# Output stage of a four-layer kernel: four tokens in a row per partition, and nine tiles for the chunks on their way out

## The reference

```python
y = (y0 + y1 + y2 + y3).transpose(0, 2, 1)
zf = jax.nn.silu(z.reshape(Bb, L, Cd))
yz = y * zf
mu = yz.mean(-1, keepdims=True)
xc = yz - mu
var = (xc * xc).mean(-1, keepdims=True)
yn = gamma * xc / jnp.sqrt(var + 1e-05) + beta
out = yn @ Wout
return out.reshape(Bb, H, W, -1)
```

## Time and profile before

| | |
|---|---|
| median of 3 runs | 3990.94 us (3986.17 to 3993.93) |
| the profiled execution | 3985.26 us, of it 3983.4 us span |
| TensorE busy, whole span | 3674.0 us (92%) |
| output stage, first transpose to last matmul | 3861.8 to 3977.4 us, 115.6 us |
| from there to the end of the span | 6.0 us |
| granted TensorE clock in the output stage | 0.99 |

### The profile page before, as it was taken

One profiled execution on the slowest core, in us unless ns is written; L12 is line 12 of the kernel. 1 busy time (PEld: TensorE's weight loads), 2 busy tenths in 40 slices (PEclk: granted clock), 3 DMA queues, 4 the chain that ended last, 5 costly groups with the idle time before them and its releaser, 6 DMA issues. The chain is left out here.

```text
span 3983.4 us, 72793 instructions
## 1 busy us (share of the span) xinstructions
PE 3674.0 (92%) x24602; PEld 2919.0 (73%) x24602; DVE 3250.2 (82%) x7827; ACT 2792.2 (70%) x6269; POOL 1342.3 (34%) x1652
## 2 busy tenths in 40 slices
PE   7999996999999999999999999998799866878898
PEld 5788774899888998889998898886576642333347
DVE  6899995777787777877778777776889988998885
ACT  5788884677776677767677766675967657777753
POOL 6799982000010000110001100003302348888873
PEclk8999997999999999999999999999999985887789
DMA  8777761000010000110001100003234446656567
GB/s 215 204 207 210 205 163 30 18 20 27 15 43 24 23 22 17 36 32 20 28 17 29 32 14 9 10 10 101 99 123 167 156 166 184 188 182 212 169 192 229
DMA packets 291428, 382.94 MB, mean 96 GB/s; under 512 B 43760, under 2 KB 162160, under 8 KB 290288
## 3 DMA queue, kind: packets, MB, share of 16 engines
q1 hardware_dynamic: 260288, 310.60, 25.6%
q0 software_dynamic: 29184, 67.27, 6.3%
q10 hardware_dynamic: 1584, 0.40, 0.1%
HBM read 205.46 MB, written 119.54 MB: 82 GB/s over the span
## 5 line engine op out<-in xcount | busy, mean ns | idle before, releaser
L959 ACT ACTIVATE l_ph<-l_T 128x512 fp32r<-128x512 f32 x1024 | 611.7, 597 | 550.4 <-PE l_T L864 550.4
L1076 DVE TENSOR_TENSOR l_pl<-l_T,l_ph 128x512 fp32r<-128x512 f32 x1024 | 707.2, 691 | 273.8 <-ACT l_ph L959 273.0
L1065 DVE CUSTOM_DVE_ANT_0 l_pr<-l_S,l_zero 128x512 f32<-128x512 f32 x1024 | 704.7, 689 | 76.4 <-PE l_S L787 12.7
L964 ACT ACTIVATE l_pr<-l_pr,l_st 128x512 f32<-128x512 f32 x1024 | 731.7, 715 | 1.1 <-DVE l_st L1071 1.0
L876 PE MATMUL l_O<-l_ph,l_vh 128*128 128x256 f32 x2048 | 661.6, 323 | 12.5 <-DVE l_pl L1076 12.1
L864 PE MATMUL l_T<-l_ident,l_pr 128*128 128x128 f32 x4096 | 612.8, 272 | 0.0
L1108 POOL TENSOR_TENSOR l_xs<-l_xs,l_bob 128x128 f32<-128x128 f32 x128 | 57.1, 460 | 1645.2 <-DMA l_xs<-x 1644.4
L864 PEld LDWEIGHTS l_T<-l_ident,l_pr 128*128 128x128 f32 x4096 | 507.8, 140 | 136.5 <-issue 0.2
L877 PE MATMUL l_O<-l_ph,l_vl 128*128 128x256 f32 x2048 | 577.9, 282 | 0.0
L878 PE MATMUL l_O<-l_pl,l_vh 128*128 128x256 f32 x2048 | 577.2, 282 | 0.0
L785 PE MATMUL l_S<-l_kh,l_qh 128*128 128x512 f32 x1024 | 417.7, 408 | 2.4 <-DVE l_st L1065 2.2
(11 more groups left out here) (269 smaller groups left out, 8025.9 us busy)
## 6 DMA issues: line engine op xcount, KB each, us to landing
l3b_u<-ub SPq DMA_DIRECT2D x256, 256.0 KB, 3.0
l_kq<-l_hl SPq DMA_DIRECT2D x192, 128.0 KB, 5.4
l_kq<-l_hl POOLq DMA_DIRECT2D x192, 128.0 KB, 4.5
zs<-l_tmp SPq DMA_DIRECT2D x64, 256.0 KB, 3.3
ub<-l3a_u SPq DMA_DIRECT2D x32, 512.0 KB, 3.4
l3b_z<-zs SPq DMA_DIRECT2D x64, 256.0 KB, 3.6
yz<-l3b_z SPq DMA_DIRECT2D x64, 256.0 KB, 3.3
l3b_dt<-yz SPq DMA_DIRECT2D x32, 512.0 KB, 4.8
```

What stands on the lines that cost most here:

```text
L959: e.activation(ph[:, i, :], psT[:, i, :], ACT.Copy).then_inc(p_hi, 1)
L964: e.activation(pr[:, s, es], pr[:, s, es], ACT.Exp, bias=st[:, s, 9:10], scale=SC, accum_out=st[:, s, 10 + k:11 + k]).then_inc(exped, 1)
L1065: e.tensor_tensor_reduce(pr[:, s, ks], psS[:, bk, :], zero[:].broadcast_to([128, 512]), 1.0, -3.0e38, ALU.add, ALU.max, st[:, s, kc:kc + 1 ...
L1076: e.tensor_tensor(pl[:, i, :], psT[:, i, :], f32(ph[:, i, :]), ALU.subtract).then_inc(p_lo, 1)
```

## The change

Three things change in the output stage.

- The four tokens of a partition become neighbours. Block j of a chunk is now the tokens j, 4 + j, 8 + j, ..., in place of 128j to 128j+127: both the transposes and the matmuls read the stationary operand as `j::4`.
- A partition's four tokens are then one row of 2 KB in `out`, and the store is 128 rows of 2 KB in place of 512 rows of 512 bytes.
- A chunk leaves from one of nine slots in place of three: three of `tE` and the six of `U` ("l3b_u"), which the scan steps have used up by then. The wait for a store, and the semaphores, go by nine.

```diff
-        M, B, N = 64 * NI, 6, 8 * NI
+        M, B, N, OUT = 64 * NI, 6, 8 * NI, 9
...
+        def o_of(f):
+
+            return tE[:, f % OUT, :] if f % OUT < 3 else U[:, f % OUT - 3, :]
...
-                    e.dma_start(out[n, 8 * c:8 * c + 8].rearrange("(t r) c d -> (r c) t d", r=2), tE[:, f % 3, :].rearrange("p (t c) -> p t c", t=4)).then_inc(o_out[f % 3], 16)
-            for i in range(3):
-                w.wait_ge(o_out[i], 16 * len(range(i, N, 3)))
+                    e.dma_start(out[n, 8 * c:8 * c + 8].rearrange("r (c t) d -> (r c) t d", t=4), o_of(f).rearrange("p (t c) -> p t c", t=4)).then_inc(o_out[f % OUT], 16)
+            for i in range(OUT):
+                w.wait_ge(o_out[i], 16 * len(range(i, N, OUT)))
...
-                            t = e.transpose(psL[:, 2 * (f % 2) + j // 2, 256 * (j % 2) + 128 * h:256 * (j % 2) + 128 * h + 128], y_of(f)[:, h, 128 * j:128 * j + 128], ident[:])
+                            t = e.transpose(psL[:, 2 * (f % 2) + j // 2, 256 * (j % 2) + 128 * h:256 * (j % 2) + 128 * h + 128], y_of(f)[:, h, j::4], ident[:])
...
-                            t = e.matmul(psC[:, f % 2, 128 * j:128 * j + 128], y_of(f)[:, h, 128 * j:128 * j + 128], gc[:, h, :], start=(h == 0), stop=(h == 1))
+                            t = e.matmul(psC[:, f % 2, 128 * j:128 * j + 128], y_of(f)[:, h, j::4], gc[:, h, :], start=(h == 0), stop=(h == 1))
...
-                    if f >= 3:
-                        w.wait_ge(o_out[f % 3], 16 * (f // 3))
+                    if f >= OUT:
+                        w.wait_ge(o_out[f % OUT], 16 * (f // OUT))
                     else:
                         w.wait_ge(added, M // 2)
                     for j in range(4):
-                        t = e.activation(tE[:, f % 3, 128 * j:128 * j + 128], psC[:, f % 2, 128 * j:128 * j + 128], ACT.Copy, scale=rs[:, f % 2, 2, j:j + 1])
+                        t = e.activation(o_of(f)[:, 128 * j:128 * j + 128], psC[:, f % 2, 128 * j:128 * j + 128], ACT.Copy, scale=rs[:, f % 2, 2, j:j + 1])
...
-                o = tE[:, f % 3, :].rearrange("p (t c) -> p t c", t=4)
+                o = o_of(f).rearrange("p (t c) -> p t c", t=4)
```

More of the change, by code:

```diff
@@ L1797, in y_of @@
             return tT[:, s:s + 2, :]
+        def o_of(f):
+            return tE[:, f % OUT, :] if f % OUT < 3 else U[:, f % OUT - 3, :]
         ident_in, wide_in, u_in, z_in, y_out = P.sem("ident_in"), P.sem("wide_in"), P.slots("u_in", 6), P.slots("z_in", 4), P.slots("y_out", 4)
         skips_in = P.slots("skips_in", 2)
-        weights, y_in, o_out = P.sem("weights"), P.slots("y_in", B), P.slots("o_out", 3)
+        weights, y_in, o_out = P.sem("weights"), P.slots("y_in", B), P.slots("o_out", OUT)
         d_full, C_full, X_full, W_full, T_full, O_full = (P.sem(x) for x in ("d_full", "C_full", "X_full", "W_full", "T_full", "O_full"))
```

## The result

The changed kernel takes 4048.07 us in the median of 4 runs against 3988.56 of the kernel before in 4: ratio 1.0142, 95% interval 1.0124 to 1.0159. That is 59.5 us slower, far outside the range of the prediction (3984 to 4020). The profiled execution has a span of 4040.5 us, 57.1 more than before.

The account below looks back on a forecast made before the run. TensorE was taken to bound the output stage, its loads as long as its matmuls. Nine tiles -6.8, 2 KB rows 0 and strided loads +19.2 gave +12.4 us on 3990.94, so 4003.3 us, range 3984 to 4020.

Parts of the forecast that it names:

- What bounds the stage: Output stage: TensorE sets the pace, busy 111.14 of 115.6 us; any slower plain load is paid at once.
- Nine tiles, -6.8 us: Output stage: nine tiles outlast any store, so the wait for it goes, worth up to -6.8 us.
- waiting for y: Chunk 31's y load: 2.0 us come back if TensorE stays as fast, none if strided loads slow it.
- 2 KB rows, 0: Output store: 128 rows of 2 KB land no sooner than 512 of 512 B; gain 0, bound half a us.
- The step that failed: Strided weight loads, output stage: L1984's strided moving rate, 1.04 ns a value, gives 133 ns a load; +19.2 us in all.
- The term of the plain loads: Output matmuls (L2034): 133 against 109 ns, +24 ns on each of 512 loads, 12.3 us.
- ScalarE's 0.85 ns on top of the plain rate: Upper bound for strided loads, from ScalarE's strided copy (L1686 against L1670): 108 ns a plain load, 70 us in all.
- The prediction's own sign, a spacing beyond 3 us: Output stage: group spacings passing 3 us would show the forecast wrong and the much slower case true.
- The term of the transposing loads: Output-stage transposes (L2025): 136 against 109 ns, +27 ns on each of 256 loads, 6.9 us.
- Rival D: Output-stage loads pay the price of ScalarE's strided copies: +70 - 6.8 = +63.6 us, 4054; chance 0.12.
- rival A: The forecast itself: strided output-stage loads at 1.04 ns a value, +12.4 us, range 3999 to 4008; chance 0.45.
- Rival B: Output-stage loads read values 16 bytes apart without slowing: -4.0 us, 3987, or -6.0, 3985; chance 0.33.

Follow-up runs that it names:

- nine_tiles: Changed kernel with contiguous loads and 512-byte store rows, so only the nine tiles differ from the kernel before: 3987.58 us against 3994.16, ratio 0.9987.
- moving4: Changed kernel with the output matmuls' operands swapped: gc stationary, y moving through with j::4, transposes reading 128 tokens in a row; 4047.49 us.
- r4_moving: Changed kernel with output matmuls on fp32r D (moving, step of four) and selwide (stationary), 8 pairs per chunk, transposes contiguous; 3972.22 us.

## Why the prediction was wrong, step by step

- *What bounds the stage* was right: TensorE, with the loads as long as the matmuls, so that a slower load is paid at once. The stage grew by what its pairs grew.
- *Nine tiles, -6.8 us* was right in size. The account of the changed kernel closes with it, and alone it gives 5.9 us, since 1.1 us of waiting for y come back (forecast 2.0). In the changed kernel no wait for y comes back, as forecast.
- *2 KB rows, 0* was right: 61.9 us of waits against 61.8, a stage 0.3 to 0.5 us longer.
- *The step that failed:* "If that is a rate of reading single fp32 values out of SBUF, a load of 128 such values takes 133 ns", and with it "I take the middle value, since it is the same engine and the same memory". The rate of 1.04 ns is that of one path: a moving operand in fp32r, which reads 0.42 ns a value when contiguous. (The trace of before shows that: after L1984's start at 3402.22 in the earlier trace rows the next group starts 0.64 us later, of which 0.43 are L2008's second pass; 0.21 us are left for 512 values.) A plain load needs 0.85 contiguous and 1.82 with one value per line; so does a moving operand in fp32, with 1.78. The term of the plain loads was 12.3 us and is 61.8. The ratio of that row, 1.04/0.42 = 2.5, applied to the plain load's 0.85, would have given 272 ns; its absolute rate gave 133. The runs gave 233, between them and nearer to the ratio. ScalarE's 0.85 ns on top of the plain rate (217 ns) was nearer still, though of another engine. The prediction's own sign, a spacing beyond 3 us, came true at 3.72.
- *The term of the transposing loads* was 6.9 us and is 2.6. They are 68 ns longer, a little less than forecast (+79), but the matmul's pass hides them almost wholly: the pair takes 119 ns and not the 136 that I built up. This error has the other sign and is far smaller than the first: the loads cost 64.4 us together, and 19.2 were forecast.
- *Rival D* had the cost nearly right (+63.6 us; its own terms add up to 63.2) for a chance of 0.12, in part by luck: 108 ns a plain load out of ScalarE's rows, where 121 were paid, and 56 a transposing one, where 10 were. The two errors, -6.5 and +11.7 us, partly cancel. Against it I had put that TensorE's own strided read paid less. It did, on another path.
- *A slip of no weight:* 28 ns a load give 4006 us by the prediction's own terms, and its range for rival A ends at 4008.
- *Rival B*, that 16 bytes are the smallest step that leaves a line and might be free, fell: 16 bytes cost about what 32 and 256 do. What is cheap is a step that stays within a line for two values (6 ns a plain pair).

Open is why a plain load and a moving fp32 operand share one rate per line and the fp32r moving operand has another. Both slow ones take 0.84 to 0.85 ns a value when contiguous, two clocks of 2.4 GHz, and the fast one takes 0.42, which is one; whether the same cause doubles their time per line was not tried.

## What to carry to other kernels

Before a layout is turned so that a store gets longer rows, look at who reads with the new step. A stationary fp32 operand that takes one value per 16 bytes took a pair of load and matmul from 112 to 233 ns here, where loads and matmuls of 128 columns fill the engine, and the stage from 109.7 us (nine_tiles) to 173. A step of two elements cost 5.2 us of the stage, nearly all that the tiles had won. A longer row is worth something only if a store's landing is what someone waits for, and here 512 bytes landed as soon as 2 KB; more tiles took the same wait away for free. When no row shows the operation itself, a rate from another path is a weak bound, even on the same engine and memory: compare first what both need when contiguous. Here 0.42 against 0.85 ns a value gave the difference away, and the ratio came nearer than the nanoseconds; that it does so elsewhere is not shown.

## What was not expected of the hardware

- The time of a plain weight load goes by the 16-byte lines that it touches, 1.7 to 1.9 ns each, once that exceeds the 112 ns of a contiguous pair (steps 2, 3, 4, 8, 64: 118, 174, 233, 238, 218 ns a pair); at step 4 fp32r pays the same (236).
- A moving operand with one value per line costs 1.78 ns a value in fp32 (moving4), but at most 0.98 in fp32r at 16 bytes (r4_moving) and 1.04 at 256 (L1984).
- The load of a transpose goes from 141 to some 200 ns at steps of 2 to 8 elements, and to 254 at 64; the pair grows from 109 only to 110 to 120 (143 at step 64).
- ScalarE's 61.8 us of waiting for stores were worth 5.9 us of the stage.
